# One transformer block on one core: the opening and the seams between batches rescheduled

## The reference

```
h  = layernorm(x)
qk = h Wqk,  v = h Wv                       # 16 heads of 16 channels
dot[h] = qk_h^T qk_h over the 2048 tokens   # 16x16 for each head
attn = softmax(tau * (2 dot - q2_i - q2_j) / sqrt(2048))
x  = x + layernorm((attn v) Wo)
h  = layernorm(layernorm(x)) * ln_g + ln_b
out = sum over the top 2 of 7 experts of gate * (silu(h W1_e) * (h W3_e)) W2_e   # capacity per expert
      + (silu(h W1s) * (h W3s)) W2s                                              # shared expert
x  = x + layernorm(out)
```

## Time and profile before

| | |
|---|---|
| median of 3 runs | 1194.78 us (1194.01 to 1196.54) |
| profiled execution | 1200.61 us |
| its span in the profile | 1198.9 us |
| TensorE busy | 1092.5 us (91%) |
| TensorE weight loads | 996.6 us (83%) |
| VectorE busy | 677.3 us (56%) |
| ScalarE busy | 514.5 us (43%) |
| GpSimd busy | 383.0 us (32%) |
| mean granted TensorE clock | 0.955 of full |

### The profile page before, as it was taken

One profiled execution on the slowest core, in us unless ns is written; L12 is line 12 of the kernel. 1 busy time (PEld: TensorE's weight loads), 2 busy tenths in 40 slices (PEclk: granted clock), 3 DMA queues, 4 the chain that ended last, 5 costly groups with the idle time before them and its releaser, 6 DMA issues. The chain is left out here.

```text
span 1198.9 us, 19328 instructions
## 1 busy us (share of the span) xinstructions
PE 1092.5 (91%) x6744; PEld 996.6 (83%) x6744; DVE 677.3 (56%) x1727; ACT 514.5 (43%) x911; POOL 383.0 (32%) x333
## 2 busy tenths in 40 slices
PE   3576999999999999999999996999999999999980
PEld 2365888888888888888888786999999999999870
DVE  5543783555783465683465642445464554645796
ACT  2323343344343334343334422546355454554564
POOL 3411444011453011453011465243443533312233
PEclk9666999999999999999999997999999999999995
DMA  4684333015333024223015425144252532336596
GB/s 149 214 332 160 106 98 120 14 53 176 106 102 128 1 68 162 107 102 128 1 63 184 143 96 184 37 121 104 60 137 42 123 98 60 78 85 192 161 347 235
DMA packets 85483, 146.13 MB, mean 122 GB/s; under 512 B 10516, under 2 KB 61848, under 8 KB 85408
## 3 DMA queue, kind: packets, MB, share of 16 engines
q1 hardware_dynamic: 69072, 117.69, 29.5%
q0 software_dynamic: 16336, 27.48, 9.2%
HBM read 76.34 MB, written 68.78 MB: 121 GB/s over the span
## 5 line engine op out<-in xcount | busy, mean ns | idle before, releaser
L1497 DVE TENSOR_TENSOR sb_act<-bank,sb_act 128x512 f32<-128x512 f32 (+2 forms) x240 | 148.7, 620 | 405.0 <-PE bank L1015 334.5
L1013 PE MATMUL bank<-sb_h_hi,sb_wup_lo 128*128 128x512 f32 (+2 forms) x960 | 354.9, 370 | 15.7 <-DVE sb_h_lo L1467 12.7
L1015 PE MATMUL bank<-sb_h_hi,sb_wup_hi 128*128 128x512 f32 (+2 forms) x960 | 352.3, 367 | 0.0
L1014 PE MATMUL bank<-sb_h_lo,sb_wup_hi 128*128 128x512 f32 (+2 forms) x960 | 351.8, 366 | 0.0
L935 ACT ACTIVATE sb_act<-bank 128x512 f32<-128x512 f32 (+2 forms) x240 | 129.8, 541 | 438.0 <-PE bank L1015 339.3
L1013 PE MATMUL bank<-sb_wdn_hi,sb_act_lo 128*128 128x256 f32 (+1 forms) x848 | 249.4, 294 | 12.4 <-DVE sb_act_lo L1473 12.0
L1015 PE MATMUL bank<-sb_wdn_hi,sb_act_hi 128*128 128x256 f32 (+1 forms) x848 | 239.3, 282 | 0.0
L1014 PE MATMUL bank<-sb_wdn_lo,sb_act_hi 128*128 128x256 f32 (+1 forms) x848 | 238.9, 282 | 0.0
L1013 PEld LDWEIGHTS bank<-sb_h_hi,sb_wup_lo 128*128 128x128 f32 x960 | 182.2, 190 | 34.3 <-DVE sb_h_lo L1467 13.4
L1015 PEld LDWEIGHTS bank<-sb_h_hi,sb_wup_hi 128*128 128x128 f32 x960 | 182.2, 190 | 22.9
L1014 PEld LDWEIGHTS bank<-sb_h_lo,sb_wup_hi 128*128 128x128 f32 x960 | 182.8, 190 | 17.8
(11 more groups left out here) (180 smaller groups left out, 1341.2 us busy)
## 6 DMA issues: line engine op xcount, KB each, us to landing
sb_xin<-in_L_ffn_W_dram SPq DMA_DIRECT2D x28, 512.0 KB
sent_scratch<-sb_act SPq DMA_DIRECT2D x8, 1548.0 KB, 21.1
sb_xin<-in_L_attn_x_dram SPq DMA_DIRECT2D x16, 512.0 KB
sb_x<-in_L_attn_x_dram SPq DMA_DIRECT2D x16, 512.0 KB
x_scratch<-sb_x SPq DMA_DIRECT2D x16, 512.0 KB, 3.7
hT_scratch<-sb_hr SPq DMA_DIRECT2D x16, 512.0 KB
sb_hfull<-hT_scratch SPq DMA_DIRECT2D x16, 512.0 KB
y_scratch<-sb_ysb SPq DMA_DIRECT2D x14, 512.0 KB, 3.4
```

The source lines that it names most:

```text
L1013: t_.matmul(o, a_lo, b_hi, start=start, stop=False, skip_group_check=True)
L1014: t_.matmul(o, a_hi, b_lo, start=False, stop=False, skip_group_check=True)
L1015: return t_.matmul(o, a_hi, b_hi, start=False, stop=stop, skip_group_check=True)
L1497: v.tensor_tensor(act[:, m % 2, 0:c.w], bank[(4 if c.wide and m % 2 else 0) + 1][:, 0:c.w], act[:, m % 2, 0:c.w], ALU.mult).then_inc(act_o ...
```

## The change

- The opening's DMAs are reordered: the residual buffers `x2` take groups 0 and 1 and `xin` takes groups 2 and 3, at once; Wv comes behind the first x group, Wqk and Wo behind all x, then three weight pieces, and Wr, ln_g, ln_b, tau last. Each engine waits only for what it needs (`wv_in`, `const_in`, `vec_in`, `tau_in`). Groups 0 and 1 are normed from `x2`.
- Two buffers for the normed x (`xn` and `ln_o`) and for its halves (`xx`, the second in `wdn_lo[1]`); batch 0's transposes go to banks 0 to 3, 6 and 7, and the low halves of groups 1 to 3 come later. In batch 0 the pieces of the shared weights are converted at places 20 to 37 instead of 9 to 28.
- The first group's h of every batch is written into `hfull` and stays there: no store and no load for it.
- Batch 0's timetable is rewritten. Chunk 0 begins behind group 0's h; group 1's o and u steps end beside it, `o_stats` of group 2 and the rest come at its places 0 and up, and `o_mix` of group 3 at place 5. Batch 1's x steps come 6 places later, its m steps at places 26 to 36 of the batch's own count instead of 20 to 37.
- No drain behind a batch: one list of 14 chunks runs through, each chunk's last two `down` calls inside the next chunk.
- The clears: two in flight, from a buffer that the first chunk doesn't use.

The diff, cut to what the steps speak of:

```diff
+        xx = [w[1][:, :, :].rearrange("p m d -> p (m d)").rearrange("p (t h d) -> p t h d", h=2, d=D)
+              for w in (wdn_hi, wdn_lo)]
...
+        xnorm = [xn, ln_o]
...
+        blank = early[:, 0:SPARE * UW]
...
+        BEFORE = PLACES - LEAD
...
+        X_STEPS = (("x_stats", 0), ("x_norm", 3), ("x_high", 4), ("x_turn0", 4), ("x_part", 5), ("x_keep0", 5),
+                   ("x_turn1", 6), ("x_gram", 7), ("x_keep1", 7))
+        X_LOWS = (("x_low0", 6), ("x_low1", 7))
...
         for q in range(GB):
...
+            put(0, -BEFORE, q, [(name, 4 * q + at) for name, at in X_STEPS])
+        put(0, -BEFORE, 0, X_LOWS)
+        put(0, -BEFORE, 2, [("x_low0", 8 + 6)])
+        put(0, -BEFORE, 0, M_STEPS_AT)
+        put(0, -BEFORE, 2, [("x_low1", 24)])
+        put(0, -BEFORE, 1, [("x_low0", 24), ("x_low1", 25)])
+        put(0, -BEFORE, 3, [("x_low0", 34), ("x_low1", 34)])
+        put(0, -BEFORE, 0, [("scale_taus", 25)])
+        for j, at in enumerate((20, 20, 25, 35, 35, 37)):
+            put(0, -BEFORE, j, [("w_first", at)])
+        for j, at in ((3, 21), (4, 22), (5, 23)):
+            put(0, -BEFORE, j, [("w_load", at)])
+        for k, at in enumerate((15, 16, 17, 18, 24, 28, 32, 36)):
+            put(0, -BEFORE, k, [("clear", at)])
+
+        for q, places in enumerate(((-14, -13, -12, -12, -11, -10, -8, -7, -6, 1, 2),
+                                    (-13, -7, -6, -4, -3, -1, 1, 3, 4, 6, 7),
+                                    (-9, 0, 2, 2, 4, 6, 8, 9, 10, 12, 13),
+                                    (5, 7, 9, 9, 11, 12, 14, 15, 16, 18, 19))):
+            put(0, 0, q, zip(O_NAMES, places))
+        put(0, 0, 0, [("h_first", -5)])
+        put_routing(0, 0, ((8, 8, 11, 11, 12), (21, 23, 26, 27, 28)), (13, 17, 33, 37))
+
+        for b in range(1, B):
+            origin = PLACES * (b - 1)
+            put(b, origin, 0, [("x_first", 0)])
+            origin += LEAD
+            for q in range(GB):
+                put(b, origin + 4 * q + (6 if b == 1 else 0), q, X_STEPS + X_LOWS)
+            put(b, origin, 0, M_STEPS_AT if b > 1 else zip([name for name, _ in M_STEPS_AT],
+                                                          (26, 27, 27, 28, 28, 29, 29, 30, 31, 31, 32, 33, 34, 34, 35, 35, 36)))
...
+        def x_bank(b, q, k):
+
+            return (0, 2, 6, 0)[q] + k if b == 0 else 6 + k
...
+            def clear(b, k):
+                if k >= 2:
+                    sp.wait_ge(none_in[k % 2], 16 * (k // 2))
+                    sp.sem_inc(sp_go, 1)
...
+            sp.dma_start(x2[:, 0, :, :], x_t[0]).then_inc(xres_in[0], 16)
+            weight(tsb, Wv, wv_in)
+            sp.dma_start(x2[:, 1, :, :], x_t[1]).then_inc(xres_in[1], 16)
+            for k in range(2):
+                sp.dma_start(xin[:, k, :, :], x_t[2 + k]).then_inc(x_in_s[k], 16)
+            for dst, src in ((wqk, Wqk), (wo, Wo)):
+                weight(dst, src, const_in)
+            for j in range(3):
+                w_load(0, j)
+            weight(wr, Wr, vec_in)
...
             def x_norm(b, q):
                 g = b * GB + q
                 dve.wait_ge(a_rstd, g + 1)
-                dve.wait_ge(xhi_ok, OPEN + g)
-                dve.wait_ge(xlo_ok, OPEN + g)
-                dve.wait_ge(xt_ps, OPEN + g * 2)
+                dve.wait_ge(xhi_ok, OPEN + g - 1)
+                dve.wait_ge(xlo_ok, OPEN + g - 1)
+                dve.wait_ge(xt_ps, OPEN + (g - 1) * 2)
...
-                    s.activation(hr[:, k, :], bank[6 + k][:, :], ACT.Identity,
+                    s.activation((hfull if q == 0 else hr)[:, k, :], bank[6 + k][:, :], ACT.Identity,
                                  scale=gcol[:, k:k + 1], bias=bcol[:, k:k + 1]).then_inc(hT_ok, 1)
...
             pe.wait_ge(const_ok, NCONST)
-            pe.wait_ge(const_in, 16 * NSMALL)
+            pe.wait_ge(wv_in, 16)
...
-            for place in range(PLACES - LEAD):
-                attend(steps, place, 0)
-            for b in range(1, B):
-                cs = [shared_chunk(b - 1, j) for j in range(GB)] + [shared_chunk(b, 0)]
-                for j in range(GB):
-                    body(cs[j - 1] if j else None, cs[j], cs[j + 1],
-                         lambda place: beside(steps, 2 * FM * j + place, b), j == GB - 1)
-                for m in (FM - 2, FM - 1):
-                    down(cs[GB - 1], m)
...
+            for place in range(-BEFORE, 0):
+                attend(steps, place)
+            cs = first_chunks()
+            for prev, c, nxt in cs:
+                body(prev, c, nxt, lambda place: attend(steps, 2 * FM * c.n + place))
...
```

More of the change, by code:

```diff
@@ L399, in sandwich_kernel @@
[L399 to L411, removed]
+        BEFORE = PLACES - LEAD
+        LAST = 2 * FM * (FIRST - GB + HELD)
+        END = 2 * FM * FIRST
+        schedule = [[] for _ in range(BEFORE + END)]
+        def put(b, origin, q, names):
+            for name, at in names:
+                schedule[BEFORE + origin + at].append((name, b, q))
@@ new lines, in sandwich_kernel, with put_routing @@
+        O_STEPS = (("o_mix", 0), ("o_stats", 1), ("o_norm", 3), ("o_apply", 3), ("o_add", 5), ("u_stats", 7),
+                   ("u_norm", 9), ("u_turn0", 11), ("u_turn1", 12), ("u_route", 14), ("u_copy", 15))
+        O_NAMES = [name for name, _ in O_STEPS]
+        R_NAMES = ("r_top", "r_next", "u_count", "u_slot", "u_place")
+        def put_routing(b, origin, pairs, firsts):
+            for pair in range(2):
+                put(b, origin, pair, zip(R_NAMES, pairs[pair]))
+            for q in range(GB):
+                put(b, origin, q, [(f"u_send{t}", firsts[q] + t) for t in range(GT)])
@@ L432, in sandwich_kernel, with attend @@
         WEIGHTS_AT = (1, 3, 5, 7, 9, 11)
         LOW_BEHIND = 2
-        def attend(steps, place, b):
-            for name, q in (ending if isinstance(b, int) and b == B - 1 else timetable)[place]:
+        def attend(steps, place):
+            for name, b, q in schedule[BEFORE + place]:
                 if name in steps:
@@ L573, in _, with shared_places @@
+            def shared_places(n):
+                b, j = n // GB, n % GB
+                for place in range(2 * FM):
+                    if place == (5 if n == 0 else 2) and j < GB - 1:
+                        load_h(b, j + 1)
+                    if place == 6 and n > 0:
+                        store_y(*divmod(n - 1, GB))
+                    attend(steps, 2 * FM * n + place)
+            for n in range(FIRST - HELD):
+                shared_places(n)
             b = B - 1
@@ L926, in take_y, with body @@
                 ins.then_inc(y_sb, 1)
-            def body(prev, c, nxt, between=lambda place: None, late=False):
+            def body(prev, c, nxt, between=lambda place: None):
                 for m in range(FM):
@@ L1544, in route, with between @@
                     indices()
-            cs = [None] + last_chunks() + [None]
-            for j in range(1, len(cs) - 1):
-                body(cs[j - 1], cs[j], cs[j + 1], lambda place: beside_last(steps, route, 2 * FM * (j - 1) + place))
-            low(cs[-2], FM - 1)
+            def between(place):
+                attend(steps, place)
+                if place >= LAST:
+                    route(place - LAST)
+            cs = first_chunks()
+            for prev, c, nxt in cs:
+                body(prev, c, nxt, lambda place: between(2 * FM * c.n + place))
+            low(cs[-1][1], FM - 1)
             prep(expert_chunk(0, 0, 1))
```

296 lines of the change are left out of this document (141 added, 155 removed).

## The result

| | before | after |
|---|---|---|
| median of the comparison | 1195.66 us (1194.01 to 1198.05) | 1162.74 us (1161.45 to 1164.06), 4 runs each |
| profiled execution | 1200.61 us | 1161.56 us |
| its span | 1198.9 us | 1159.8 us |
| mean granted TensorE clock | 0.955 | 0.974 |

The ratio is 0.9728, 95% interval 0.9712 to 0.9745: 2.7% faster, 32.9 us in the comparison, with 1165.0 forecast.

The account below looks back on a forecast made before the run. The opening was bound by a chain over all engines, the rest by TensorE from chunk 0. Terms -31.0 + 6.0 + 1.5 - 6.6 + 0.2 = -29.9 us took the median 1194.8 to 1164.9, stated as 1165; range 1157 to 1177.

Parts of the forecast that it names:

- 1, first x group: Opening: x group 0 loaded as the first DMA, there at about 6.2 us; VectorE's statistics begin earlier, gain 6.5 us.
- 2, last Gram call's end: Opening's loop over x groups: the last Gram call ends at 32.5 us instead of 43.11; gain 10.6 us (7.9 to 12.1).
- 3, m steps: Opening, last Gram call to first mix: 24.1 us as before, so o_mix 0 begins at 56.6 us.
- 4, first mix to chunk 0: Opening, o_mix 0 to chunk 0: 21.2 us instead of 41.6, gain 20.4 us; chunk 0 begins at 77.8 us.
- 5, left behind: Work moved beside chunk 0: 6.0 us of TensorE's time plus 1.5 us of waits for VectorE (0 to 12).
- 6, seams: Batch ends: three pairs of TensorE waits, 6.6 us in all, go when down calls have an up between them.
- 7, batch 1's m steps: Batch 1's m steps in 10 places instead of 17: cost 0.2 us, range 0 to 4.
- larger-gain rival: Opening with shorter gaps and more upper clock, Gram calls and m products 6 us faster together: 1159 us; chance 0.09.
- The rule against the row: Weight pieces beside the m steps: GpSimd and VectorE may exclude each other; 1.5 us could be lost, 0 taken.
- One of my signs: Behind chunk 0's start: under 3 us of TensorE idle in 55 us would show the prediction right.
- slower rival: Chunk 0: gaps of moved steps hold TensorE at the lower clock, costing 36 us, time 1201 us; chance 0.03.
- rival in which VectorE holds chunk 0: Chunk 0: moved steps queue on VectorE ahead of products up waits for; gain only 19.4 us, time 1175; chance 0.15.

Follow-up runs that it names:

- the control of the last group: The changed kernel once more, unaltered, beside the last group's runs: 1161.63 us, ratio 0.9724 to the kernel before; its profiled execution 1165.02 us.

## Why the prediction was right, step by step

| step | forecast | the first profile |
|---|---|---|
| 1, first x group | 6.2 us | 6.80 |
| 2, last Gram call's end | 32.5 | 33.26 |
| 3, m steps | 24.1 | 22.5 |
| 4, first mix to chunk 0 | 21.2 | 19.2 |
| chunk 0 begins | 77.8 | 74.93 (75.58 and 77.68 in the other two) |
| 5, left behind | +7.5 | +10.0 |
| 6, seams | -6.6 | -9.7 |
| 7, batch 1's m steps | +0.2 | 0 |
| mid-run delays of before's profile | 0 | -2.3 |
| behind the gather | 0 | -3.2 |

**Steps 1 to 4** held. The 31.0 us forecast were 33.9, 33.3 and 31.2 in the three profiles of the changed kernel; what varies is the clock of the m steps and of the mixes. In the first profile mix 0 ran at the upper level (2.4 GHz), 0.12 us a matmul, and the transposes of u took 1.09 us for the 1.97 of the earlier trace rows. This is the larger-gain rival in part: 2 to 3 us, not 6. What I had as one reason in step 2, the second buffers, was no reason there by its run; the order of the loads and no piece beside a norm carried it by theirs (6.2 and 5.2 us), and what the low halves left out are worth stays open.

**The rule against the row.** I took 0 for the pieces beside the m steps. The row says 2.27 us where 0.42 was before: 1.85 us, above my bound of 1.5 and within the estimate from the Trainium skill, "SBUF — State Buffer", section "Who interferes with whom", which has a two-input VectorE operation and a GpSimd operation exclude each other for a whole instruction. The rule was the better guide, and the row of 3.21 us in the earlier trace rows had said the same. My reason, that some pieces had stood beside these steps before, was a reason about places in a timetable, not about times in the trace. It cost little: the control with the lower clock lost only 0.5 us to the same piece (0.91 us for L1345), and freeing the chain altogether changed no median.

**Step 5** was mis-sized: the moved work is 5.5 us by starts for 6.0, and the waits are 5.8 us where I took 1.5 of a range to 12. That the sum is over by 2.5 only is partly that chunk 0 ran less at the lower clock (1.3), which I had not counted. One of my signs failed with it: 3.4 us of TensorE idle in the 55 us behind chunk 0's start, where I wanted under 3. The busy share of VectorE (35.16 of 51.07 us) had said nothing of it. The waits are not for the product L1497, as I had them, but most of them (4.7 of 5.8 us) for the operands of the transposes, the last instructions of a chain that goes through GpSimd.

**Step 6** was mis-sized the other way: 6.6 forecast; 9.7 between the profiles, and 8.6 to 11.5 by the two kernels that put the drains back. I had added the idle rows. They count from the modelled end of the matmul before, and leave out the later wait of `u_count` (L1190 in that run).

**Step 7** cost nothing; the lead is 23.9 us from the middle of chunk 2 through chunk 3.

**The rest.** The last two lines of the table, 5.5 us, were not forecast, and I take them not to belong to the change: the delays come and go with the group of runs, and the stretch at the lower clock behind the gather, 13.7 us in the profile of before and 10.2 in that of after, with the execution (10.2, 6.8 and 10.2 in the three profiles of the changed kernel; of the kernel before one profile was read, so for it that is argued). Taken off, 39.1 becomes 33.6, and the medians part by 32.9. So the sum to compare with the forecast gain of 29.9 is some 33.5: the forecast was too small by 2.9 in the opening and by 3.1 at the seams, too large by 2.5 behind chunk 0, and the 0.2 of step 7 did not come. That the forecast missed the median by 2.3 us is partly luck: these cancel. The slower rival did not come: the clock was 0.97 through chunk 0. The rival in which VectorE holds chunk 0 was right in kind, at a quarter of its price in the net (2.5 for 10.5 us).

## What to carry to other kernels

Price a gap between two stages from the starts of the instructions around it, not from the idle row. When a chain on several engines is moved beside work that fills TensorE, look at the last link before TensorE and not at the busy share of its engine. Keep large GpSimd operations away from VectorE operations on a critical chain, by their times in the trace; the norms, with one large input, were held as the two-input products were.

## What the runs showed of the hardware that I had not expected

Between executions of one kernel the granted clock can differ in the same stretch, here one in which TensorE is about half idle: 24 matmuls in 4.77 us at 1.00, or in 6.71 us at 0.67, and with it 2.7 us at chunk 0. Behind the gather the stretch at the lower level was 13.7, 10.2, 6.8 or 3.4 us long in the profiles of these kernels.

A VectorE operation beside a GpSimd one does not slow down evenly: with a piece starting 0.36 us ahead of it `m_diag` took 2.27 us, with one 1.7 us ahead 0.91. In both cases it ends 0.28 us behind the piece's end (42.66 and 42.38; 43.27 and 42.99), as if it had waited for it. The second pair, from the control of the last group:

```profile
42.36 0.91 DVE L1345 TENSOR_TENSOR sb_hr<-sb_hr,sb_ident 128x256 f32<-128x256 f32 x1 [4.59 <-ACT sb_hr L873]
...
40.65 2.34 POOL L722 TENSOR_TENSOR sb_wup_lo<-sb_ysb,sb_wup_hi 128x1024 fp32r<-128x1024 f32 x1 [0.61 <-ACT sb_wup_hi L947]
```

A VectorE operation of four columns with a piece beside it did the same (1.23 us for 0.17).

The waits put to "remote" and the delays with them are in every profile of two groups and in none of the third; of the three profiles of the changed kernel one has them. So they go with the chip or the hour and not with the kernel. What they are stays open.
